# A Gram matrix on 128 columns of TensorE, or on two halves of 64 columns

## The reference

```
# layer 0: channel attention
q = x.reshape(b, c, h * w)
att = jnp.einsum('bcn,bdn->bcd', q, q)              # the Gram matrix, 64 x 64 for each image
rev = jnp.max(att, axis=-1, keepdims=True) - att
res = jnp.einsum('bcd,bdn->bcn', softmax(rev), q)
x = gamma * res + x
# layer 1 and layer 3: a long convolution in both directions with separable filters
out = irfft2(rfft2(x) * k_f)[..., :L, :L] + x * bias[:, None, None]
# layer 2: Haar transform, two products over the channels with soft threshold, inverse transform
f1 = haar2d(x)
for i in range(2):
    f4 = jnp.einsum('bchw,oc->bohw', f1 * v[i], conv_w[i])
    acc = acc + jnp.sign(f4) * relu(jnp.abs(f4) - tau[i])
x = haar2d(acc, inverse=True) + x
```

## Time and profile before

| | |
|---|---|
| median of three runs | 6691.49 us |
| the profiled execution | 6684.96 us, its span 6683.2 us |
| PE busy | 6293.8 us, 94% |
| PEld, DVE, ACT, POOL busy | 82%, 60%, 58%, 38% |
| share of the chain that ended last: PE | 89% |
| of it line 435, the Gram matmuls | 6% |
| mean granted clock of TensorE | 0.976 of full speed |
| DMA | mean 182 GB/s |

### The profile page before, as it was taken

The page is one execution under the profiler, slowest core; times in us unless marked ns, Lnnn a source line. Parts: engine busy times, 40 slices in busy tenths (PEclk is TensorE's granted clock), DMA queues, the critical chain, the costliest instruction groups (busy, mean ns, idle before and its releaser), DMA issues.

```text
span 6683.2 us, 142217 instructions
## 1 busy us (share of the span) xinstructions
PE 6293.8 (94%) x37984; PEld 5492.5 (82%) x37984; DVE 4013.7 (60%) x7165; ACT 3907.3 (58%) x7001; POOL 2554.8 (38%) x2436
## 2 busy tenths in 40 slices
PE   6798799999999999999999999999999999999689
PEld 4495599788988899888998889978898889989579
DVE  1142377556775577655776467755676558866866
ACT  1233466555665566655665556655566557755865
POOL 0000255224552255423553235522455226632952
PEclk9898899999999999999999999999999999999999
DMA  6776655575656656476655756656565665534224
GB/s 193 227 214 213 201 187 186 181 223 178 186 178 201 206 183 187 156 239 189 186 185 171 238 173 186 186 183 218 178 186 177 202 202 168 168 120 140 80 83 129
DMA packets 770829, 1217.29 MB, mean 182 GB/s; under 512 B 78854, under 2 KB 475047, under 8 KB 770568
## 3 DMA queue, kind: packets, MB, share of 16 engines
q1 hardware_dynamic: 623112, 945.68, 48.1%
q10 hardware_dynamic: 147456, 268.50, 10.6%
HBM read 808.13 MB, written 405.73 MB: 182 GB/s over the span
## 4 chain that ended last, share of the span: by engine, by line
PE 89%; DMA 4%; ACT 2%; DVE 2%; issue 2%; POOL 1%; SPq 1%; ACTq 0%; DVEq 0%; POOLq 0%
PE ps L457 26%; PE ps L459 13%; PE ps L524 12%; PE ps L475 8%; PE ps L483 7%; PE ps L467 7%; PE ps L435 6%; PE ps L601 5%; DMA mixed<-x 3%; PE ps L535 3%; PE ps L649 1%; DMA pix<-in_x_pix 1%; ACT x L762 1%; DVE pix L1011 1%; DVE ps L1026 1%
## 5 line engine op out<-in xcount | busy, mean ns | idle before, releaser
L1045 POOL TENSOR_TENSOR mag<-mag,sgn 128x512 f32<-128x512 f32 x896 | 1041.5, 1162 | 2177.5 <-ACT mag L714 2151.7
L1060 POOL TENSOR_TENSOR split_a<-field,split_a 128x512 fp32r<-128x512 f32 x512 | 652.0, 1274 | 1798.8 <-ACT split_a L774 1798.8
L457 PE MATMUL ps<-tab_a,img 128*128 128x256 f32 x4096 | 1234.0, 383 | 6.9 <-issue 6.2
L457 PE MATMUL ps<-tab_b,mid 128*128 128x256 f32 x4096 | 1223.3, 380 | 0.4 <-DVE x L940 0.4
L905 DVE TENSOR_TENSOR held<-ps,v_t 128x512 f32<-128x512 f32 x896 | 619.7, 692 | 650.8 <-PE ps L524 609.6
L459 PEld LDWEIGHTS ps<-tab_a,img 128*128 128x128 f32 x4096 | 785.4, 192 | 109.6
L459 PEld LDWEIGHTS ps<-tab_b,mid 128*128 128x128 f32 x4096 | 778.2, 190 | 105.1
L459 PE MATMUL ps<-tab_a,img 128*128 128x128 f32 x4096 | 791.9, 275 | 0.0
L459 PE MATMUL ps<-tab_b,mid 128*128 128x128 f32 x4096 | 786.8, 274 | 0.0
L457 PEld LDWEIGHTS ps<-tab_a,img 128*128 128x128 f32 x4096 | 705.6, 193 | 83.0 <-issue 7.4
L475 PE MATMUL ps<-s_inv,split_a 128*128 128x256 f32 x4096 | 710.0, 317 | 66.5 <-POOL split_a L1060 37.7
(11 more groups left out here) (98 smaller groups left out, 11131.1 us busy)
## 6 DMA issues: line engine op xcount, KB each, us to landing
pix<-in_x_pix SPq DMA_DIRECT2D x256, 512.0 KB, 3.9
mixed<-x ACTq DMA_DIRECT2D x512, 256.0 KB, 3.1
img<-mixed SPq DMA_DIRECT2D x512, 256.0 KB, 2.7
tab_a<-filt SPq DMA_DIRECT2D x1024, 128.0 KB, 2.8
tab_b<-filt SPq DMA_DIRECT2D x1024, 128.0 KB, 2.8
coef<-res ACTq DMA_DIRECT2D x512, 256.0 KB, 2.0
out<-res SPq DMA_DIRECT2D x512, 256.0 KB, 3.2
pix<-in_x_rows SPq DMA_DIRECT2D x128, 512.0 KB, 4.8
```

The source lines that it names most:

```text
L457: nc.tensor.matmul(o_ps, src[:, 0, H * half:H * half + H], tab[:, N - 1::-1], start=True, stop=False)
L1045: nc.gpsimd.tensor_tensor(mag[:, a], mag[:, a], sgn[:, a], ALU.mult).then_inc(c_mult, 1)
L1060: nc.gpsimd.tensor_tensor(split_a[:, 1], src, split_a[:, 0].bitcast(F32), ALU.subtract)\
```

## The change

Each matmul of a whole tile, 128 stationary columns and 128 moving columns, becomes two: for `e` = 0 and 1 the 64 columns of pixel group `e` are the stationary and the moving operand, and the result goes to partitions 64e to 64e+63 of the bank, columns 0 to 63. The output partitions are the array's columns, so `e` = 0 lies in the first half of them and `e` = 1 in the second. Nothing is computed any more of the two blocks that were never read. `att_copy` reads both blocks from columns 0 to 63. The matmuls on zeros in `gram_edge` and everything else stay as they are.

```diff
                 for j in range(j0, j0 + count):
-                    mm = nc.tensor.matmul(ps[:, 7, 0:2 * C], pix[:, buf, j, :], pix[:, buf, j, :],
-                                          start=False, stop=False, skip_group_check=True)
+                    for e in range(2):
+                        own = pix[:, buf, j, C * e:C * e + C]
+                        mm = nc.tensor.matmul(ps[C * e:C * e + C, 7, 0:C], own, own,
+                                              start=False, stop=False, skip_group_check=True)
                 return mm
...
                 for e in range(2):
-                    ins = nc.vector.tensor_copy(att_s[C * e:C * e + C, :], ps[C * e:C * e + C, 7, C * e:C * e + C])
+                    ins = nc.vector.tensor_copy(att_s[C * e:C * e + C, :], ps[C * e:C * e + C, 7, 0:C])
                 ins.then_inc(att_copied, 1)
```

## The result

The changed kernel took 6812.62 us (median of 4 runs, 6808.77 to 6818.41). The kernel before, measured beside it, took 6688.95 us (4 runs, 6683.74 to 6696.54). The ratio is 1.0185 with a 95% interval of 1.0167 to 1.0202: slower by some 124 us, where 318 had been forecast.

A forecast was written before the change was run, and what follows sets the result against it. PE was taken to bound the forward steps; 0.015 for passes, 0.145 in and 0.195 out made 0.355 us per group, times 896 +318 us, so 7003, stated as 7010 us (+4.8%). Range: 6795 to 7045, 8 times in 10.

The forecast's parts named there:

- The bound: Forward steps: PE never idle, Gram passes wholly in the chain, so each gain or loss per group counts 896 times.
- The change of form: Around each forward-step Gram group: switching between 128 and 64 columns drains PE, 0.145 us in and 0.195 us out.
- C: Gram groups: a mere change of columns drains nothing and the halves run side by side, -193 us, 6500; chance 0.05.
- D: Inside each Gram group: every change of half drains too, +390 us on top, 7400; chance 0.04.
- The passes themselves: Inside a Gram group: eight half-column passes one after another at 0.0575 us, 0.46 us against 0.445, +0.015 us.
- rival B: Gram groups: passes of the two halves overlap, eight in 0.23 us, +112 us with drains, 6805; chance 0.26.
- A: Gram groups: passes one after another, a drain in and out, 7010, own range 6985 to 7040; chance 0.60.
- The first image: First image's Gram passes: 1.84 us of work instead of 1.8, hidden under the wait for tile DMAs, costing nothing.
- something else slower: Whole kernel: an unlisted slowdown, for example a clock that falls in the pauses; chance 0.02.
- signs named for the profile after: Expected: 8192 Gram records, groups about 0.6 us, loads 0.07 us early, following group 0.2 us more, shrink step 0.71 us longer.

The follow-up runs named there:

- experiment 6: Kernel before the change, whole-tile matmuls kept, but the eight tiles of a DMA in one group every second step: 6696.83 us, ratio 1.001.
- experiment 2: Kernel before the change, plus one 64-column matmul on zeros ahead of each two-tile group in the forward steps: 7094.63 us, ratio 1.0602.
- experiment 1: Changed kernel, but both 64-column matmuls of a tile write to partitions 0 to 63, the same half of the columns: 7017.11 us, ratio 1.0482.
- experiment 7: Changed kernel with the two loops swapped: in each two-tile group four passes of one half, then four of the other: 6810.97 us, ratio 1.0175.

## Why the prediction was right or wrong

**The bound was right.** PE bound the Gram stages without a gap, and every change in a group's length came out at the end in full: by the chain +0.13 us for each group (0.38 - 0.445 + 0.195), times 896, is 116 us of the 124 measured. Of the rest the two profiled executions tell a part. In each of the six shrink stages the time from the first Gram matmul to the last grew alike, and here is the first of them, before and after (duration min/median/max, then first and last start):

```profile
L435 PE MATMUL ps<-pix x512: 272/275/275, 756.6 to 1197.3; 128*128 128x128 f32 x171
```

```profile
L437 PE MATMUL ps<-pix x1024: 222/222/271, 781.0 to 1238.1; 128*64 128x64 f32 x171
```

That is 440.7 and 457.1 us, +16.4, which is the 0.13 of 128 groups within rounding. The stage without shrink grew by 19.1 (306.1 to 325.2); from 280 to 290 us it ran at granted clock 0.72, in place of 1.00. From its last Gram matmul to the first of the next stage it took 5.3 us more, which I don't assign. What is left of the 125.7, some 3 us, is within the scatter: ten runs of experiment 6's kernel lie up to 20 us apart.

**The change of form was right, with its size.** 0.145 in and 0.195 out had been taken from neighbours (rows of lines 447 and 494), and experiment 2 gives 0.145 and 0.19 to 0.20 without the split tiles; the 0.61 us of experiment 1, less eight turns of 0.058, leave 0.146 for the way in too. The exit of a 128-row, 64-column form, which could have been anything from 0 to 0.20, is at the top; no row showed that, and taking the nearest row was a choice that came out. What gave the way in away ahead of time was one distance, 0.07 us from load to the modelled end of the matmul ahead, in every place where the form changed. The rule of the Trainium skill (TensorEngine Tiling (Array Packing), Key Properties), that a change of mode drains TensorE and a change of tile within one does not, agrees with the traces in both its halves: C and D are both out.

**The step that failed is "The passes themselves".** I took 0.0575 us a pass, 0.46 for eight. Eight passes hold 0.38 - 0.145 = 0.235 us, 0.029 each: half. I had priced just this as rival B, at 6805, and 6812.62 came, but gave it 0.26 against 0.60 for A. The argument that tipped it was false. From two loads 0.055 us apart I concluded that loads keep in line, and so that matmuls side by side would gain nothing. But those two loads went to the same columns. A row of one resource used twice says nothing on two resources, and with both halves in use loads go two at a time, just as matmuls do (experiment 1 against the changed kernel: 0.54 and 0.31 us for eight loads). The second argument, that no load of the trace ever started before the matmul ahead of it, had the same fault: in the trace all of them needed the same columns. For a thing that no row shows I should have let the two cases stand nearly even, with the point between them, or given more weight to what the prediction quotes from the Trainium skill (TensorE: Matmul & The Clock Gate, Part 3) for column tiles side by side, 2.38 times with three of them. With two halves this case's traces agree: eight passes in 0.235 us, against 0.61 - 0.145 = 0.465 when all lie in one half.

**The first image cost nothing, as forecast, but not for the reason given.** The prediction counted 32 passes at full clock, one after another, under a wait of 1.1 us. In fact the clock fell there; the prediction had a falling clock only as an example inside its 0.02 for something else slower. The passes of the two halves, side by side, made up for it (2.00 us at half the clock against 2.07 before). The one error paid for the other, and that is luck.

**The range** held, since it had been drawn to take in both A and B. The direction held too, and does not hang on the failed term: groups of two tiles lose with B as with A. The break even follows from the measured terms. A tile costs 0.223 us whole (two passes of 0.1115) and 0.118 in halves (two pairs of 0.059), so it saves 0.105; a group pays 0.34. It takes 3.2 tiles to pay for a change of form and back. Two tiles lose 0.13 us (measured +124 us in all), four win 0.08 (x 448 = 36, measured 31), eight win 0.50 (x 224 = 112, measured 103), sixteen 1.34 (x 112 = 150, measured 148). The prediction had all but one of these terms, and never asked how large a group would have to be.

**Of the signs named for the profile after**, these came: 8192 records of line 437 in the new form, loads 0.07 us ahead of the modelled end, and 0.2 us more on what is behind a group. The sign of B, passes some 0.03 us apart, came as well, and a step grew by 0.27 us, not 0.71.

## What to carry to other kernels

Using half of the array's columns twice over halves the time of a small matmul only if both halves are really at work, and each change between a full and a half form cost a fixed 0.34 us there and back here. So count the groups, not the matmuls: put enough narrow matmuls behind one another (here more than three tiles), and alternate the halves in program order. When the trace lacks the case, a row in which one resource is used twice in a row is an upper bound for two resources, not an estimate.

## What the runs showed of the hardware that was not expected

- Loads of weights into the two halves of the columns run at the same time: eight in 0.31 us, against 0.54 us when all go to one half.
- A float32 pass of 64 stationary and 64 moving columns takes a turn of 0.058 to 0.059 us, and two in different halves share one turn.
- Passes of different halves need not start in the order of the program, but the reach is small: three passes overlapped at each change of half in long blocks (29 and 23 turns for 32 passes), four of four at the start of a group (experiment 7).
- A change of the columns in use from 128 to 64 costs 0.145 us and back 0.19 to 0.20 us, with the rows left at 128, even where the narrow matmul between adds only zeros (experiment 2).
- Where PE waits for DMAs between its groups, the side-by-side passes left it less busy (60.38 us of 90 against 69.29), and the granted clock fell from 1.00 to a mean of 0.65; with the same narrow passes all in one half (experiment 1) PE was busy 68.60 us in that stretch and the clock was 0.94. Busy time alone doesn't tell it: the kernel of experiment 7 was busy 62.27 us there, and its clock was 0.94 too.
